# A fused cross-attention and routed-FFN kernel: results added straight into the output rows, last logits handed over on chip, a different order for the first expert

## The reference

```
x = x + cross_attention(ctx_768, layernorm(x), mask, ...)
x = x + routed_ffn(layernorm(x), ...)

routed_ffn(x):                      # 4096 tokens, 16 experts
  xn     = x / rms(x) * norm_weight
  logits = xn @ router_weight.T + router_bias          # 4096 x 16
  probs  = softmax(logits)
  idx    = top_k(logits.T, 256)     # each expert takes its 256 best tokens
  y      = gelu(xn[idx] @ fc1.T + b1) @ fc2.T + b2
  output[idx]    += y * probs[idx]
  gate_sums[idx] += probs[idx]
  output = output / gate_sums where gate_sums > 0
```

## Time and profile before

| | us |
|---|---|
| median of 3 runs | 1271.85 (1271.23 to 1273.03) |
| profiled execution, own time | 1276.79 |
| span of its profile | 1275.0 |
| PE busy | 1055.4 (83%) |
| DVE busy | 813.9 (64%) |
| POOL busy | 794.9 (62%) |
| ACT busy | 629.4 (49%) |

### The profile page before, as it was taken

The page is one execution under the profiler, slowest core; times in us unless marked ns, Lnnn a source line. Parts: engine busy times, 40 slices in busy tenths (PEclk is TensorE's granted clock), DMA queues, the critical chain, the costliest instruction groups (busy, mean ns, idle before and its releaser), DMA issues.

```text
span 1275.0 us, 17549 instructions
## 1 busy us (share of the span) xinstructions
PE 1055.4 (83%) x6105; PEld 649.8 (51%) x6105; DVE 813.9 (64%) x1897; ACT 629.4 (49%) x1209; POOL 794.9 (62%) x876
## 2 busy tenths in 40 slices
PE   3669999999999999999999999883112899999980
PEld 2535446446445545545544644332011788888870
DVE  2666777767768867867776787603577466666524
ACT  5636665665665766666576554441000433333331
POOL 3207876885895896796797697890101466666642
PEclk9859999999999999999999999996555899999995
DMA  9110010110110020011100100101600296665628
GB/s 272 37 42 1 17 38 1 34 39 2 45 46 2 1 68 23 1 52 39 36 1 6 35 2 3 34 2 39 223 0 10 97 289 192 176 177 175 178 58 270
DMA packets 77672, 88.06 MB, mean 69 GB/s; under 512 B 26496, under 2 KB 71568, under 8 KB 73488
## 3 DMA queue, kind: packets, MB, share of 16 engines
q1 hardware_dynamic: 64624, 77.47, 18.7%
q0 software_dynamic: 6144, 8.67, 4.1%
q10 hardware_dynamic: 6816, 0.80, 0.5%
HBM read 65.13 MB, written 21.79 MB: 68 GB/s over the span
## 4 chain that ended last, share of the span: by engine, by line
PE 62%; DVE 16%; POOL 9%; issue 6%; DMA 3%; ACT 3%; SPq 1%; POOLq 0%; ACTq 0%; DVEq 0%
PE bank L626 49%; PE pair_bank L626 8%; POOL prob_sum L1142 8%; DVE y_out L1531 3%; DVE hot_ids L1494 3%; DVE above_trial L1423 3%; ACT probs L890 2%; PE bank L699 2%; PE bank L651 1%; DMA acc_scratch<-squares 1%; DVE y_out L1528 1%; POOL z_lo L1121 1%; DVE masked_scores L1340 1%; DVE hot_lo L1492 1%; DVE hot_hi L1491 1%
## 5 line engine op out<-in xcount | busy, mean ns | idle before, releaser
L1142 POOL TENSOR_TENSOR prob_sum<-prob_sum,probs 128x256 f32<-128x256 f32 x640 | 475.6, 774 | 83.7 <-ACT probs L890 77.6
L1340 DVE CUSTOM_DVE_ANT_0 masked_scores<-pair_bank,mask_bias 128x512 bf16<-128x512 f32 x256 | 166.4, 688 | 84.6 <-PE pair_bank L626 84.4
L890 ACT ACTIVATE probs<-bank,mask_col 128x512 f32<-128x512 f32 x256 | 162.2, 686 | 114.4 <-PE bank L626 113.2
L626 PE MATMUL bank<-probs,v_nat 128*64 128x512 f32 x768 | 205.5, 617 | 0.4 <-ACT probs L890 0.4
L1164 POOL TENSOR_TENSOR w_lo<-w_raw,w_hi 128x1024 fp32r<-128x1024 f32 x32 | 85.0, 2656 | 94.6 <-ACT w_hi L890 94.6
L1333 DVE TENSOR_REDUCE maxima<-pair_bank 128x2 f32<-128x1024 f32 x64 | 78.3, 1223 | 47.5 <-PE pair_bank L626 47.5
L626 PE MATMUL pair_bank<-k_hi,q_hi 64*128 64x512 f32 x384 | 93.8, 482 | 13.6 <-DVE maxima L1340 9.0
L626 PE MATMUL bank<-q_hi,k_hi 64*128 64x512 f32 x384 | 94.8, 486 | 10.7 <-ACT probs L890 8.8
L890 ACT ACTIVATE probs<-bank 128x512 f32<-128x512 f32 x128 | 69.5, 595 | 66.0 <-PE bank L626 64.6
L1142 POOL TENSOR_TENSOR prob_sum<-probs 128x256 f32<-128x256 f32 x64 | 44.8, 731 | 83.7 <-ACT probs L890 70.5
L1370 DVE RECIPROCAL bank<-bank 128x128 f32<-128x128 f32 x64 | 58.6, 944 | 60.1 <-PE bank L626 60.1
(11 more groups left out here) (209 smaller groups left out, 2536.3 us busy)
## 6 DMA issues: line engine op xcount, KB each, us to landing
w_raw<-in_fc SPq DMA_DIRECT2D x16, 1024.0 KB, 4.8
w<-in_fc SPq DMA_DIRECT2D x16, 1024.0 KB, 5.6
c_in<-in_ctx SPq DMA_DIRECT2D x16, 384.0 KB, 3.4
acc_scratch<-squares SPq DMA_DIRECT2D x4, 1028.0 KB, 15.8
x_in<-in_x SPq DMA_DIRECT2D x8, 512.0 KB, 4.9
x_scratch<-x_in SPq DMA_DIRECT2D x8, 512.0 KB, 3.5
rows_scratch<-xr_nat SPq DMA_DIRECT2D x8, 512.0 KB, 3.7
x_back<-x_scratch SPq DMA_DIRECT2D x1, 4096.0 KB, 21.5
```

The source lines that it names most:

```text
L626: return pe.matmul(out, lhsT, rhs, start=start, stop=stop, skip_group_check=True)
L890: return act.activation(out, a, f, bias=bias, scale=scale)
L1142: last = tt(total[:, half], first[:, half], p[:, half], ALU.add)
L1340: last = dve.tensor_tensor_reduce(masked_scores[:, hh, :], pair_bank[:, hh, :], mask_bias[:, 512 * g:512 * (g + 1)], 1.0, MASKED, ALU.add, ...
```

## The change

- The attention result x2 is stored directly to the output, and each scatter adds rows of 256 floats into the output (`out_rows`). The clearing of `acc_scratch`, the reload of x2, and the whole last stage are gone. POOL waits for the last two scatters instead.
- To make plain sums right, the gates are divided by each token's gate sum beforehand (`scale_gates`, DVE, five operations on all 4096 by 16). The scaled gates are stored twice: to `gates_scratch`, from which the first three experts fetch their gates by separate gathers of 16-float rows (`gather_gates`), and over the gate columns of `rows_scratch` (`renew_rows`, once the gathers of experts 0 to 2 have landed), for which `gather` of experts 3 and up waits.
- Each half of an expert is scattered by its own plan step (`scatter(e, c)`). For experts 0 to 14 both stand at the place of the old one; for the last expert each stands behind its own `gate`.
- The logits of batches 0 to 5 are loaded for the search before attention ends; those of batches 6 and 7 go from SBUF straight into the search's tile. The search's small tiles lie in the context input buffers, so DVE and PE begin it without waiting for the other engines.
- Counts and `same_expert` are bfloat16 (counts less 256). Constants for the order step are made during the middle round.
- `slots` is cut into `order(part)` and `slots(part)`, part 0 for expert 0 alone, part 1 for the other 15, with fewer operations (no integer conversions).
- Expert 0 has an order of its own (`first_expert`), and the weights of experts 0 and 1 are both split before the search. The lists of experts 3 and 4 come during expert 1.
- ACT loads its tables only after the stores of attention have landed, and loads all gate probabilities too.

```diff
+    def first_expert():
+        add("order", 1)
+        add("turn_tokens", 0)
+        add("slots", 1)
+        add("list_hot", 1)
+        for f in range(FT):
+            add("hidden", 0, f)
+            if f == 4:
+                add("list_count", 1)
+                add("list_join", 1)
+            elif f == 5:
+                add("list_spread", 1)
+                add("gather", 1)
+                add("scale_gates")
+                add("list_hot", 2)
+                add("gather_gates", 0)
+                add("gather_gates", 1)
+        for c in range(2):
+            for f in range(FT):
+                add("expert_out", 0, c, f)
+                if c and f == 3:
+                    add("list_count", 2)
+                    add("list_join", 2)
+                elif c and f == 5:
+                    add("list_spread", 2)
+                    add("gather", 2)
+                    add("gather_gates", 2)
+                    add("renew_rows")
+            add("gate", 0, c)
+            if c == 0:
+                add("turn_tokens", 1)
-    run(split(0))
+    for e in range(2):
+        run(split(e))
     add("search")
-    add("slots")
-    for e in range(2):
-        run(list_tokens(e))
-        add("gather", e)
-    add("turn_tokens", 0)
+    add("order", 0)
+    add("slots", 0)
+    run(list_tokens(0))
+    add("gather", 0)
+    first_expert()
...
         def store_chunk(b):
             on.wait_ge(*misc.emptied("route_logits", b))
-            sync.dma_start(chunks_dram[b * E:(b + 1) * E, :], logits_T).then_inc(chunk_stored, 16)
+            if b == DIRECT:
...
+                sync.dma_start(logits_by_chunk[0:DIRECT * E, :], chunks_dram).then_inc(search_loaded, 16)
+            to = chunks_dram if b < DIRECT else logits_by_chunk
+            sync.dma_start(to[b * E:(b + 1) * E, :], logits_T).then_inc(chunk_stored, 16)
...
+        def scale_gates():
+            settle(stt(taken_probs[:], slot[:], float(CAP - NO_SLOT), all_probs[:].rearrange("p j e -> p e j"),
+                       ALU.is_lt, ALU.mult))
+            settle(dve.tensor_reduce(gate_sum[:], taken_probs[:].rearrange("p e j -> p j e"), AX, ALU.add))
+            settle(stt(gate_sum[:], gate_sum[:], 0.0, gate_sum[:], ALU.is_le, ALU.add))
+            settle(dve.reciprocal(inv_sum[:], gate_sum[:]))
+            tt(all_probs[:], all_probs[:], inv_sum[:].unsqueeze(2).broadcast_to([P, NT, E]),
+               ALU.mult).then_inc(gates_scaled.sem, 1)
...
+        def gather_gates(e):
+            on.wait_ge(gates_stored, 16)
+            for c in range(2):
+                pool.indirect_dma_start(
+                    gate_rows[e][:, c, :], None, gates_dram,
+                    bass.IndirectOffsetOnAxis(ap=token_index[e][:, c:c + 1], axis=0)).then_inc(gate_gathered[e], 16)
...
-        def scatter(e):
+        def scatter(e, c):
             i = e % 2
-            on.wait_ge(*gated.at(e, 1))
-            on.wait_ge(acc_cleared, 16 * N_CLEAR)
+            on.wait_ge(*gated.at(e, c))
+            on.wait_ge(x2_stored, 16 * B)
             if e:
                 on.wait_ge(scatter_done[(e - 1) % 2], 32 * ((e - 1) // 2 + 1))
...
+            if e < EARLY:
+                on.wait_ge(gate_gathered[e], 32)
+                value = gate_rows[e][:, c, e:e + 1]
+            else:
+                value = gathered[e % GATHERS][:, c, D + e:D + e + 1]
+            ts(y_out[i][:, c, :], y_out[i][:, c, :], value, None, ALU.mult).then_inc(gated.sem, 1)
...
+            elif kind == "scale_gates":
+                on.wait_ge(*gates_scaled.at())
+                sync.dma_start(gates_dram.rearrange("(j p) e -> p j e", p=P), all_probs[:]).then_inc(gates_stored, 16)
+            elif kind == "renew_rows":
+                for early in range(EARLY):
+                    on.wait_ge(gather_done[early], 32)
+                sync.dma_start(rows_dram.rearrange("(j p) d -> p j d", p=P)[:, :, D:ROW],
+                               all_probs[:]).then_inc(rows_renewed, 16)
```

More of the change, by code:

```diff
@@ L283, in schedule_experts @@
             add("gate", e, c)
-        if e == 1:
-            add("x2_back")
-    add("scatter", E - 1)
+            if e == E - 1:
+                add("scatter", e, c)
     return plan
@@ L335, in _build @@
     mask_col = sb("mask_col", [P, B * CT], F32)
+    c_in = [sb(f"c_in{i}", [P, 4, 2 * P], F32) for i in range(2)]
     attention = ExitStack()
@@ L617, in _build @@
         searched.will("round", r)
-    for piece in (("limits",), ("order", 0), ("totals",), ("order", 1)):
-        searched.will(*piece)
+    searched.will("limits")
+    for part in range(2):
+        for piece in (("order", part, 0), ("totals", part), ("order", part, 1)):
+            searched.will(*piece)
+    experts_of = (slice(0, 1), slice(1, E))
+    order_bank, total_place = bank[5:7], slice(P, P + E)
     def tensor_program(pe):
@@ L877, in expert_out @@
                 last.then_inc(y_filled.sem, 1)
-        work = {"search": search, "slots": slots, "list_count": list_count, "list_spread": list_spread,
+        work = {"search": search, "order": order, "list_count": list_count, "list_spread": list_spread,
                 "turn_tokens": turn_tokens, "hidden": hidden, "expert_out": expert_out}
@@ L1419, in vector_program @@
         dve.drain().then_inc(attention_done, 1)
-        on.wait_ge(attention_done, 4)
         def count_at_least(i):
-            return dve.tensor_scalar(above_trial[i][:], logits_by_chunk[:], trial[:, i:i + 1].bitcast(F32), None,
-                                     ALU.is_ge, ALU.add, accum_out=count[:, i:i + 1])
+            with nc.allow_low_precision("a count less 256 is a whole number from -256 to 256"):
+                return dve.tensor_scalar(above_trial[i], logits_by_chunk, trial[:, i:i + 1].bitcast(F32), -float(CAP),
+                                         ALU.is_ge, ALU.add, accum_out=count[:, i:i + 1])
@@ L1443, in search @@
+            settle(dve.memset(kept, 0))
             for r, (first, n) in enumerate(rounds[1:], 1):
@@ new lines, in order @@
+        def order(part):
+            experts = experts_of[part]
+            columns = slice(experts.start * NT, experts.stop * NT)
+            limits = limit[:, experts].unsqueeze(2).broadcast_to([P, experts.stop - experts.start, NT])
+            flat = lambda t: t[:].rearrange("p e j -> p (e j)")[:, columns]
+            if part == 0:
+                dve.tensor_copy(wide[:], trial[0:E, 0:1].bitcast(F32).broadcast_to([E, P])).then_inc(order_ready.sem, 1)
+                on.wait_ge(*searched.at("limits"))
+                settle(dve.tensor_copy(limit[:], bank[1][:, 0:E]))
```

320 lines of the change are left out of this document (126 added, 194 removed).

## The result

| | before | after |
|---|---|---|
| median | 1272.44 us (1271.23 to 1273.32, 4 runs) | 1229.88 us (1228.26 to 1233.07, 4 runs) |
| ratio of the two | | 0.9669, 95% interval 0.9645 to 0.9694 |
| profiled execution, own time | 1276.79 us | 1228.32 us |
| span | 1275.0 us | 1226.5 us |

The change saves 42.6 us by the medians. 1226 us were forecast, in a range of 1214 to 1242.

What follows compares the result with a forecast made beforehand. PE was taken to bound the expert stage, with the chain through the idle handover, search and end deciding the gain; terms summed to -46.6 us, own time 1230.2, median 1225.3, said as 1226, range 1214 to 1242.

Steps and rivals of the forecast that it cites:

- Handover: Attention's last result to the search's first count: last logits go to SBUF, so counting starts near 892.0; -9.9 us.
- Rounds and splits: Search: 17 rounds each 0.33 shorter with bfloat16 counts, -5.6; expert 1's earlier weight split stalls DVE, +1.6.
- Slots: From `limit` to the first `hot_hi`: about 13 operations on 32 columns for expert 0 alone; -10.4 us.
- Order beside the gather: Ordering the other 15 experts during expert 0's gather makes the transposes wait 0.5 longer; +0.5 us.
- Expert 0: First matmul to expert 1's: late gate rows hold DVE, then PE at the list join; +5.6, plus +2.0 for PE's clock.
- Experts 2 to 14: Same order with a one-column copy gone from DVE's chain; -0.5 us for all.
- that rival: Faster scatters: 1024-byte rows issue like gathers, removing over half of PE's idle time per expert; 7 less, 1219, chance 0.12.
- Start: ACT loses its 0.94 wait for the clearing DMAs at the beginning; -0.9 us.
- End: Last scatter lands at 1244.1 where the span ended at 1275.0, reading back, dividing and storing gone; -30.9 us.
- that the end doesn't go: Rival that the last stage's time stays; no way seen for it, given no chance of its own.
- the tables: Rival: the early search waits for its tables, landing at 931 rather than before 921; 1236 us, chance 0.07.
- The small-row store: Gate store of 4096 64-byte rows taken at 5.5 us; rival slow stores, 34 each, gives 1274, chance 0.03.

Runs made afterwards that it cites:

- e2_f32_counts: Changed kernel with the counts and `same_expert` in float32 again instead of bfloat16; 1233.49 us, ratio to before 0.9697.
- e6_split_late: Changed kernel with expert 1's weight split moved from before the search into expert 0's hidden blocks; 1233.40 us, ratio to before 0.9676.
- e7_slots_first: Changed kernel with order and slots of the other 15 experts put before expert 0's list; 1238.18 us, ratio to before 0.9729.
- e8_gates_free: Changed kernel without the six early gate gathers and DVE's wait for them (output not the reference's); 1227.45 us, ratio to before 0.9668.
- e3_clear_back: Changed kernel with the four 1 MB clearing DMAs and the second squares' wait for them back; 1232.00 us, ratio to before 0.9667.
- e4_sp_waits_last: Changed kernel with SP instead of POOL waiting for the last scatters; 1226.85 us, ratio to before 0.9627.
- e5_three_stores_last: `e4_sp_waits_last` with three small SP stores, one after the other, behind the last scatter's landing; 1228.52 us, ratio to before 0.9650.
- e10_list1_later: `e9_both` with list 1 counted one hidden block later and its spread and gather moved into expert 0's first output half; 1224.05 us, ratio to before 0.9612.
- e1_gate_late: Changed kernel with expert 0's first gate moved on DVE behind list 2; 1229.00 us, ratio to before 0.9648.
- e9_both: Changed kernel with `e4_sp_waits_last`'s edit, gates scaled earlier, list 1 counted a block later, first gate behind list 2; 1226.93 us, ratio to before 0.9655.
- the first repeat: Changed kernel run again unchanged, beside the first three experiments; 1229.18 us.
- the second: Changed kernel run again unchanged, beside `e8_gates_free` and `e9_both`; 1228.85 us, ratio to before 0.9658.

## Why the prediction was right, and where it missed

The forecast for the median, 1225.3 (said as 1226), lies 4.6 below the measured one. By its steps:

- **Handover**: right, -9.9 against -10.05.
- **Rounds and splits**: right as a sum, -4.0 both, by luck: two misses cancel. The rounds gave 0.38 to 0.39 each and not 0.33, 6.5 in all; the stalls beside POOL cost 3.9 (1.8 and 2.1) where one pair had cost 1.6 before. `e2_f32_counts` shows that the two terms are tied. Also lacking in the prediction is that the early split has a value: `e6_split_late` puts it at 3 us net.
- **Slots**: right, -10.4, and `e7_slots_first` shows that it is the arithmetic of the other 15 experts that left the chain. A small misreading did no harm: two of the 17 operations, the scans, took 1.22 and 1.23, more than the 1.01 given as the most.
- **Order beside the gather**: +0.2 for +0.5.
- **Expert 0**: the chain was right link by link: gate row late, DVE held, PE held by the join. It cost 3.6 and not 5.6, since the store landed in 4.6 instead of 5.5 and the gather in 2.2 instead of 3.1. The clock fell once more behind PE's wait, from 983 to 987, and expert 1 took +3.9, as forecast. But that nearly all of this is the gates' price (7.6 of the forecast 9.5) is wrong: without any gate path (`e8_gates_free`) only 1.9 to 2.4 of the two experts' excess of 7 goes. As far as the timelines show, the rest comes from the fourth list, from waits for lists whose DVE steps meet POOL's splits, and from the clock behind such waits; no run takes these away one by one.
- **Experts 2 to 14**: -1.5 for -0.5. An expert took 15.4 us before, not the 15.8 that the prediction had from a stretch of more than ten. The scatters stayed at 1600 ns, so that rival fell, and with it the size of the rows as the reason: an adding scatter costs 0.46 more to issue than a gather in both kernels.
- **Start**: "Between 0 and -0.94: take -0.9" took the wrong end. ACT's wait went and came back as waits for PE; `e3_clear_back` gives 0.7 at most, not told from nothing.
- **End**: the step that failed. "lands 3.8 later [...], at 1244.1. The span ended at 1275.0: -30.9" took the landing for the end of the span. It gave -24.8. The 6.1 us are POOL's end of program, its DRAIN of 5.78 us behind the wait for the landing and what is around it. The trace of before had it too (1269.45 to 1275.0), beside SP's last stores. The sign given for it, a span that ends within 5 us of the last scatter's issue, failed likewise: it ended 10.0 us after it. In the rival "that the end doesn't go" I wrote that nothing follows the last scatter but a wait; something does.

The size of the other rivals: the tables landed by 911.5 and were asked for at 915.4, later than wished but in time. The small-row store landed in 4.6, not in 34. Eight times the rows cost 4.6 against the 1.8 of 512 in the earlier trace rows.

The misses add up: 6.1 for the end and 0.9 for the start too much gain, against 2.0 for expert 0, 1.0 for experts 2 to 14 and 0.5 for order and handover too little. That leaves 3.5 of the 4.6, so the total is as near as it is partly because misses went both ways. Of the rest, 0.5 is the median of before, 1272.44 with the later run and 1271.85 then, and 0.6 is what the stretches (-43.1) and the medians (-42.6) differ by.

## What to carry to other kernels

- Find the last act of every engine, what its queue does behind it, and the distance from each to the end of the span. A gap in which nothing works is a term of its own; here it was POOL's DRAIN, and letting SP wait for the last scatter took 2.3 us off for moving two lines.
- When one wait of PE is removed in a stretch with several short chains, ask what comes due next: with the late gate, and even with no gate wait at all, most of what expert 0 gained was given back in expert 1, by DVE instructions queued late or held beside a POOL split and by the clock behind PE's new wait.
- Price a step that is moved at both places, the one that it leaves too.

## What the runs showed of the hardware

- The span ends 5.6 to 6.3 us after POOL's last act (issue or wait), in the kernel before, in the changed one and in `e4_sp_waits_last`, and work of SP of some 4.2 us fits beside it with 0.9 us of added time (`e5_three_stores_last`). What is left of POOL's DRAIN behind that act is 5.3 us in the two kernels that issue 64 indirect DMAs (before, `e8_gates_free`) and 5.8 in those that issue 70 (the changed kernel, its repeats, `e4_sp_waits_last`). This fits a time of some 0.08 us for each, an estimate from these two counts; no run was made to test it.
- The low level of PE's clock (0.50, 1.2 GHz) comes back among the experts for some 3 to 7 us behind short stops of PE, with products of 0.41 instead of 0.28 us: behind waits of 3.93 (changed kernel), 3.18 (`e10_list1_later`), 2.48 (`e8_gates_free`), 1.94 (`e1_gate_late`), 1.90 and 1.79 (`e9_both`). Behind waits of 1.77 (changed kernel, before 1000.06), 1.43 (`e8_gates_free`), 0.99 and 0.44 (`e10_list1_later`) it did not, but nor did it behind the same wait of 1.90 in the first repeat and 1.79 in the second. So the length of the wait alone does not decide it.
- DVE instructions are held beside POOL's `w_lo` for up to its whole length: 2.09 for 0.29, 2.38 for 0.23, 2.85 for 0.68, 2.16 for 0.35. Which instruction meets it depends on the moment, as the cast of `e2_f32_counts` shows.
- A load of 4096 rows of 64 bytes blocked ACT at its issue for 12.26 us while 4 MB of weights were being loaded, and it landed after 16.6. The like load just ahead of it was issued in 0.46 and landed after 15.0, so it was the second in a row that stood; whether the weights or the load ahead held it was not tested. The similar store by SP, after the weights, was issued in 0.38 and landed after 4.6.
